# Attention with a routed MoE on one core: x and the high parts first, root chains ahead of v, unit loads in two transfers a head, and the later norms in steps 23 to 33

## What is computed

```python
x = L0_attn_x                                  # (4, 1024, 128), 16 heads of 8
xn = _layernorm(x, axis=-1)
# attention: one projection is query, key and value at once
p = jnp.einsum('bsd,ed->bse', xn, Wv) + bv     # q = k = v = p by heads
attn = softmax(q @ k.T / math.sqrt(8))
s = jnp.einsum('bsd,ed->bse', attn @ v, Wo) + bo
# ffn of xn: layernorm z (g, b), 8 experts, the best 2 of softmax(z @ rW + rb), weights renormalised
hid = gelu(z @ W1[e] + b1[e]); outs = hid @ W2[e] + b2[e]
ffn = xn + sum_e w[e] * outs[e]
out = x + s * silu(ffn)
```

## Time and profile before

| what | us |
|---|---|
| median of 3 runs | 629.17 |
| lowest, highest | 628.30, 630.58 |
| the profiled execution | 632.46 |
| its span, first to last instruction | 630.7 |
| busy: TensorE / ScalarE / VectorE / GpSimd | 571.2 / 543.2 / 240.1 / 230.1 |

### The profile page before, as it was taken

One profiled execution on the slowest core, in us unless ns is written; L12 is line 12 of the kernel. 1 busy time (PEld: TensorE's weight loads), 2 busy tenths in 40 slices (PEclk: granted clock), 3 DMA queues, 4 the chain that ended last, 5 costly groups with the idle time before them and its releaser, 6 DMA issues.

```text
span 630.7 us, 11527 instructions
## 1 busy us (share of the span) xinstructions
PE 571.2 (91%) x3990; PEld 232.3 (37%) x3990; DVE 240.1 (38%) x695; ACT 543.2 (86%) x591; POOL 230.1 (36%) x252
## 2 busy tenths in 40 slices
PE   3778884799999999799999999999988999999996
PEld 2553320223344344333444344434334343433221
DVE  5553863573333333113222232223232852223381
ACT  4576663699999999979999999999999999999994
POOL 2364047827777774254211121112203334341000
PEclk9977776799999999869999999999995999999999
DMA  6137697746466655227363445453233654442220
GB/s 164 45 101 219 231 304 276 184 132 149 110 162 133 162 96 116 70 67 160 68 153 99 127 112 132 103 135 108 70 117 108 173 167 139 130 116 83 65 66 19
DMA packets 100989, 81.54 MB, mean 129 GB/s; under 512 B 54219, under 2 KB 92638, under 8 KB 100318
## 3 DMA queue, kind: packets, MB, share of 16 engines
q1 hardware_dynamic: 94270, 71.26, 43.2%
q0 software_dynamic: 6656, 9.48, 4.8%
HBM read 58.07 MB, written 28.39 MB: 137 GB/s over the span
## 4 chain that ended last, share of the span: by engine, by line
PE 74%; ACT 9%; DVE 7%; issue 5%; DMA 4%; SPq 1%; ACTq 0%; DVEq 0%
PE bank_v L1330 35%; PE pair L1276 16%; PE bank_f L1370 8%; PE bank_f L1379 8%; ACT exps L776 7%; DMA p_dram<-w_ring 3%; PE bank_f L1347 2%; PE pair L1236 1%; ACT pre L752 1%; PE bank_f L1343 1%; PE pair L1227 1%; DMA x_tok<-in_L_attn_x 1%; DVE o_turned L1082 1%; PE bank_f L1354 1%; DVE v_tok L863 1%
## 5 line engine op out<-in xcount | busy, mean ns | idle before, releaser
L776 ACT ACTIVATE exps<-pair 128x1024 f32<-128x1024 f32 x512 | 488.9, 1049 | 54.6 <-PE pair L1276 36.3
L1330 PE MATMUL bank_v<-exps,v_tok 128*32 128x512 f32 x2048 | 285.0, 630 | 3.1 <-ACT exps L776 1.6
L687 POOL DMA_INDIRECT o_dram<-o_ring,slot_place x80 | 77.4, 968 | 238.3 <-DVE o_ring L1133 238.0
L1276 PE MATMUL pair<-q_ring,k_ring 26*128 26x512 f32 x1024 | 152.9, 513 | 2.7 <-ACT exps L776 2.1
L1276 PEld LDWEIGHTS pair<-q_ring,k_ring 26*128 26x128 f32 x1024 | 60.7, 188 | 93.4 <-ACT exps L776 54.8
L672 POOL DMA_INDIRECT z_dram<-pre,dest_i x64 | 64.3, 1004 | 52.2 <-DVE place_i L1037 33.3
L1379 PEld LDWEIGHTS bank_f<-w_ring,pre 128*128 128x128 f32 x320 | 46.2, 208 | 72.2 <-issue 43.3
L1124 DVE TENSOR_TENSOR pre<-bank_f,w_ring 128x256 f32<-128x256 f32 x80 | 33.9, 423 | 102.1 <-PE bank_f L1370 102.1
L1379 PE MATMUL bank_f<-w_ring,pre 128*128 128x128 f32 x320 | 62.5, 322 | 9.7 <-ACT pre L752 5.3
L1133 DVE TENSOR_TENSOR o_ring<-bank_f,w_ring 128x128 f32<-128x128 f32 x80 | 23.2, 290 | 124.3 <-PE bank_f L1379 121.1
L679 POOL DMA_INDIRECT place_dram<-token_place,place_i x64 | 61.3, 958 | 19.5 <-issue 19.5
(11 more groups left out here) (154 smaller groups left out, 287.1 us busy)
## 6 DMA issues: line engine op xcount, KB each, us to landing
w_ring<-w_dram SPq DMA_DIRECT2D x80, 192.0 KB
w_ring<-w_dram SPq DMA_DIRECT2D x80, 129.0 KB
q_ring<-p_dram SPq DMA_DIRECT2D x56, 104.0 KB
k_ring<-p_dram SPq DMA_DIRECT2D x56, 96.0 KB
z_dram<-s_tok SPq DMA_DIRECT2D x4, 1280.0 KB, 13.1
z_ring<-z_dram SPq DMA_DIRECT2D x80, 64.0 KB
rows_in_sb<-o_dram SPq DMA_DIRECT2D x16, 256.0 KB, 2.9
p_dram<-z_ring SPq DMA_DIRECT2D x8, 256.0 KB, 2.9
```

What stands on the lines that cost most here:

```text
L687: pool.indirect_dma_start(o_dram[:, :], bass.IndirectOffsetOnAxis(slot_place[:, h, 4 * k + i:4 * k + i + 1].bitcast(U32), 0), o_ring[:, q ...
L776: nc.scalar.activation(exps[:, g % ES, 2 * half:2 * half + 2, :], pair[(2 * g + half) % 3][:, :, :], ACT.Exp, scale=SCALE).then_inc(exp_do ...
L1276: ins = nc.tensor.matmul(pair[h % 3][:, j % 2, :], k_ring[32 * j:32 * j + KROWS, n % 2, kt * P:(kt + 1) * P], q_ring[32 * j:32 * j + KROWS ...
L1330: ins = nc.tensor.matmul(bank_v[32 * j:32 * j + 32, :], v_tok[:, (n // HG) * KT + kt, first:first + 32], exps[:, g % ES, j, :], start=(kt ...
```

## The change

SP loads x's third chunk ahead of the small weights. `sum_gram` takes no statistics between its operations, and the third `norm1` stands ahead of the first `keep_p`. `norm2` moves from between `keep_p(4)` and `keep_p(5)` to behind VectorE's branch, ahead of `keep_router_bias`. The second four warm-up matmuls go. For blocks 0 and 1 the high part is stored three times, straight into all its places, so the copy inside DRAM leaves out batch 0 and stands behind both `zero_z`. Units 0 and 1 are loaded with two transfers a head, behind the stores of blocks 3 and 4. The loads of rb, W1 and bo stand behind all stores of parts. The tables put the count in step 8, the biases in 9 to 16, the norms in 23, 25, ... 33, and the first `up` stays in step 38.

```diff
-WARM = (4, 4)
+WARM = 4
-RANK_AT = ((2, 3, 3, 4, 4, 5), (17, 18, 19, 20, 22, 23))
-COUNT_AT = (7, 24)
-ASSIGN_AT = ((7, 8, 8, 9, 10), (25, 26, 27, 28, 30))
+RANK_AT = ((3, 4, 4, 5, 5, 6), (17, 18, 19, 20, 22, 23))
+COUNT_AT = (8, 24)
+ASSIGN_AT = ((8, 9, 9, 10, 11), (25, 26, 27, 28, 30))
...
-BIAS_AT = 4
+BIAS_AT = 9
+COPY_HI_AT = 14
-NORM_AT = 12
-ZERO_AT = 12
-SCALE_W1_AT = (13, 14, 15, 16)
-SCATTER_AT = (11, 31)
-MOE_AT = 37
+NORM_AT = 23
+ZERO_AT = 8
+SCALE_W1_AT = (18, 19, 20, 21)
+SCATTER_AT = (12, 31)
+MOE_AT = 38
...
-        place(("norm", g), NORM_AT + g - EARLY)
+        place(("norm", g), NORM_AT + 2 * (g - EARLY))
...
             load_x(1)
+            load_x(2)
...
-                for part in range(PARTS):
-                    row = (HI_ROW, LO_ROW)[part]
-                    sp.dma_start(p_dram[:, row:row + DK, tokens], (p_hi, p_lo)[part][:, g % 2, :]).then_inc(parts_stored[g % 2], 16)
-                if g == EARLY:
+                hi_rows = (0, HI_ROW, LO_ROW + DK) if g < EARLY else (HI_ROW,)
+                for row in hi_rows:
+                    sp.dma_start(p_dram[:, row:row + DK, tokens], p_hi[:, g % 2, :]).then_inc(parts_stored[g % 2], 16)
+                sp.dma_start(p_dram[:, LO_ROW:LO_ROW + DK, tokens], p_lo[:, g % 2, :]).then_inc(parts_stored[g % 2], 16)
+                if g == 2:
...
+                elif g == 3:
...
-                    for j in range(4):
-                        load_head(0, 0, j, 0, kq_in[0])
-                        load_stabiliser(0, j, kq_in[0])
-                if g == 3:
-                    sp.dma_start(w1_stage, W1.rearrange("e h f -> h e f")).then_inc(w1_staged, 16)
-                    sp.dma_start(rb_bc[:, :], ...
-                    sp.dma_start(bo_bc[:, :], ...
+                    load_unit(0)
+                elif g == 4:
+                    load_unit(1)
+            sp.dma_start(rb_bc[:, :], ...
+            sp.dma_start(w1_stage, W1.rearrange("e h f -> h e f")).then_inc(w1_staged, 16)
+            sp.dma_start(bo_bc[:, :], ...
+            zero_z(0)
...
-            zero_z(0)
-            load_unit(1)
...
-                if g == 2:
+                if g == COPY_HI_AT:
                     for row in (0, LO_ROW + DK):
-                        sp.dma_start(p_dram[:, row:row + DK, :], p_dram[:, HI_ROW:HI_ROW + DK, :]).then_inc(hi_copied, 16)
+                        sp.dma_start(p_dram[:, row:row + DK, EARLY * BLK:], p_dram[:, HI_ROW:HI_ROW + DK, EARLY * BLK:]).then_inc(hi_copied, 16)
...
-                                             head_sel[:, :].unsqueeze(2).broadcast_to([P, H, DK]), ALU.mult), statistics)
+                                             head_sel[:, :].unsqueeze(2).broadcast_to([P, H, DK]), ALU.mult))
...
-            keep_p(0)
             norm1(2, *NORMS[2])
-            for g in range(1, NB):
+            for g in range(NB):
                 keep_p(g)
...
-                elif g == 4:
-                    norm2()
...
+            norm2()
             keep_router_bias()
...
-                keep_warm(WARM[1])
                 prologue()
```

More of the change, by code:

```diff
@@ L41 @@
 PARTS = 2
+EARLY_PARTS = 4
 PROWS = 3 * DK
@@ L58 @@
 PART_LOADS = 4 * 4
-KQ_FIRST = PART_LOADS + 4
+EXACT_LAST = PART_LOADS + 2 * 4
 KQ_LOADS = 4 * 2
@@ L388, in build, with stored @@
         out_rows = out.rearrange("b s d -> (b s) d")
+        def stored(g):
+            return 16 * (EARLY_PARTS + g // 2 * PARTS)
         def written(*use):
@@ L410, in _ @@
             sp.dma_start(rw_sb[:, :], rW).then_inc(small_in, 16)
-            for c in range(2, len(X_CHUNKS)):
+            for c in range(3, len(X_CHUNKS)):
                 load_x(c)
@@ L442, in load_stabiliser, with load_unit @@
                              p_dram[(n % HG) * 4 + j, M_ROW:HEAD_ROWS, tokens]).then_inc(loaded, 16)
+            def load_unit(n):
+                if n >= 2:
+                    sp.wait_ge(pv_done, (n - 1) * US)
+                if n == HG:
+                    sp.wait_ge(hi_copied, 32)
+                    for i in range(2):
+                        sp.wait_ge(m_kept[1 + i], (NB - EARLY) // 2 * 16)
+                tokens = slice((n // HG) * S, (n // HG + 1) * S)
+                for j in range(4):
+                    head = (n % HG) * 4 + j
+                    sp.dma_start(k_ring[32 * j:32 * j + PROWS, n % 2, :].bitcast(F32), p_dram[head, 0:PROWS, tokens]
+                                 ).then_inc(kq_in[n % 2], 16)
+                    sp.dma_start(q_ring[32 * j:32 * j + KROWS, n % 2, :].bitcast(F32), p_dram[head, HI_ROW:HEAD_ROWS, tokens]
+                                 ).then_inc(kq_in[n % 2], 16)
             for g in range(NB):
@@ L453, in _ @@
                         sp.dma_start(p_dram[:, M_ROW, e * BLK:(e + 1) * BLK], m_blk[:, e, :]).then_inc(m_kept[0], 16)
-                    for i in range(2):
-                        sp.wait_ge(parts_stored[i], 16 * PARTS)
+                elif g == 3:
+                    for e in range(EARLY):
+                        sp.wait_ge(parts_stored[e], stored(e))
                     sp.wait_ge(m_kept[0], 16 * EARLY)
@@ L458, in _ @@
                     sp.wait_ge(ring_cleared, 1)
-                    for j in range(4):
-                        load_head(0, 0, j, 0, kq_in[0])
-                        load_stabiliser(0, j, kq_in[0])
-                if g == 3:
-                    sp.dma_start(w1_stage, W1.rearrange("e h f -> h e f")).then_inc(w1_staged, 16)
-                    sp.dma_start(rb_bc[:, :], rb.rearrange("(a d) -> a d", a=1).broadcast_to([P, E])).then_inc(bias_in, 16)
-                    sp.dma_start(bo_bc[:, :], bo.rearrange("(a d) -> a d", a=1).broadcast_to([P, D])).then_inc(bias_in, 16)
+                    load_unit(0)
+                elif g == 4:
+                    load_unit(1)
+            sp.dma_start(rb_bc[:, :], rb.rearrange("(a d) -> a d", a=1).broadcast_to([P, E])).then_inc(bias_in, 16)
+            sp.dma_start(w1_stage, W1.rearrange("e h f -> h e f")).then_inc(w1_staged, 16)
+            sp.dma_start(bo_bc[:, :], bo.rearrange("(a d) -> a d", a=1).broadcast_to([P, D])).then_inc(bias_in, 16)
+            zero_z(0)
             for i in range(2):
-                sp.wait_ge(parts_stored[i], NB // 2 * 16 * PARTS)
+                sp.wait_ge(parts_stored[i], stored(NB - 2 + i))
             sp.wait_ge(m_row_ready, 1)
@@ L479, in _ @@
             with sp.If(m2_bits > M2_LIMIT_BITS):
-                sp.wait_ge(kq_in[0], 16 * KQ_FIRST)
+                for i in range(2):
+                    sp.wait_ge(kq_in[i], 16 * KQ_LOADS)
                 with sp.Fori(0, NU // 2) as w:
@@ L492, in _ @@
                     load_head(0, 0, j, 0, exact_in)
[L493 to L514 removed]
+                    for n in range(2):
+                        load_stabiliser(n, j, exact_in)
+                sp.wait_ge(exact_in, NU * 16 * PART_LOADS + 16 * EXACT_LAST)
             def load_w1(q):
@@ L656, in split @@
                 if g >= 2:
-                    pool.wait_ge(parts_stored[g % 2], g // 2 * 16 * PARTS)
+                    pool.wait_ge(parts_stored[g % 2], stored(g - 2))
                 pool.tensor_copy(hi.bitcast(F32R), src).then_inc(pool_chain, 1)
@@ L892, in beside_norm @@
                     keep_m2()
-                else:
-                    statistics()
+                statistics()
             for t in range(7):
```

29 lines of the change are left out of this document (4 added, 25 removed).

## The result

The changed kernel takes **644.03 us** (median of 4 runs, 641.55 to 644.75) against 629.04 us for the kernel before (4 runs, 628.3 to 630.58): a ratio of 1.0221 with a 95% interval of 1.0186 to 1.0255. It is slower by some 15 us, where 2 us faster was forecast, and outside the range of 618 to 634.5. Medians are of all executions; the ratios leave out three that took over 1.5% longer than the fastest of their kernel at a lower mean clock (two of e12's eleven, one of e9's six). The profiled execution took 644.17 us, its span is 642.4 us against 630.7, so the two traces lie 11.7 us apart; the other 3.3 us of the 15 are there because the profiled execution of the kernel before was 3.4 us over its median. 11.0 of the 11.7 us are there when the first expert product, up(0,0), starts. I read the trace along the same marks as before.

A forecast was written before the change was run, and what follows sets the result against it. Bound by 256 steps of two exponentials each, with gains only ahead of that; 21.8 us gained by step 29, mostly given back in SP's queue: 4.4 minus 2.4 leaves 2.0 us, so 627.2 us, range 618 to 634.5.

The forecast's parts named there:

- the stream behind norm 5: SP's in-order issues from VectorE's read of the last norm to up(0,0): 32.4 us, leaving TensorE waiting 16.3 us.
- how much there was to give back: The lead of the steps ahead of up(0,0): step 29 starts at 113.9 instead of 135.72, 21.8 us gained.
- rconst comes at 58.5: VectorE's router bias, waiting for bo_bc issued at 53 and landing in 5.6 us: 58.5 instead of 59.96.
- 19.5 us, and 2.4 us for the slow clock: Steps 9 to 16: eight bias uses at 2.44 us a step, plus slow clock and VectorE's long assign part.
- Steps 17 to 29: Twelve free steps (22.3 us), three norms at 0.38 us and 1 us for turn, projection and count: 24.4 us.
- the prologue: Ahead of the step loop: waits of ScalarE (4.81 us) and TensorE (4.63 us) go, step 0 starts at about 42.5.
- the lower bound that I had named: Gain at m2 from loading x sooner, put at 1.5 us: nothing if small loads land late behind x.
- the restart behind up(0,0): TensorE resumes at half clock after its wait for z_ring, costing 2.4 us.
- the warm-up: Prologue matmuls removed: transposes start at about 14.6 instead of 18.07; 2.08 us taken whole, about 1 by the skill's rule.
- up(0,0) after 155: Sign that the forecast is wrong and C or D holds: the first expert product starts later than 155 us.
- C: Rival: slower, SP's stream from norm 5's read to z outlasts the steps' lead; 632 to 634 us, chance 0.20.
- D: Rival: prologue does not move, four stores a slot hold GpSimd, bo_bc lands 3 us later; 630 to 632, chance 0.08.

The follow-up runs named there:

- e12: The changed kernel with the bias uses at steps 12 to 18 and 20 and W1's scaling at 21 to 24: 630.49 us over 11 runs, ratio 0.9993.
- e9: e5 with the bias uses at steps 12 to 18 and 20, W1's scaling and the w1 loads later: 606.50 us, ratio 0.9593.
- e1: The changed kernel with W2's copies and the places issued right behind the copy of the high parts (step 14): 630.00 us, ratio 0.9978.
- e5: The changed kernel with W2's copies, the places, rb and bo early, and w1 and z issued ahead of unit 3: 611.93 us, ratio 0.9707.
- e2: The changed kernel with the loads of rb and bo issued ahead of block 0's parts: 634.20 us, ratio 1.0054.
- e7: The changed kernel with W2's copies, the places, rb and bo early, and the matmuls of the eight bias uses left out: 612.81 us.
- e11: e5 with the bias uses at every second step (10 to 22, then 25), W1's scaling and w1 loads later: 610.46 us, ratio 0.9693.
- e13: The same kernel as e12, run under a second name for a second trace, whose execution took 632.22 us.
- e8: The changed kernel with the norms back at steps 17, 18, 20, 22, 23, 25: 632.53 us, ratio 1.0015.
- e14: e9 with m_blk's stores behind block 1's parts and unit 0's loads behind block 2's: 604.86 us, ratio 0.961.

## Why the prediction was wrong, step by step

**Right: the stream behind norm 5.** Forecast 32.4 us from VectorE's read of norm 5 to up(0,0); measured 165.68 - 132.34 = 33.3. Forecast 16.3 us of wait, 12 to 20; measured 19.6. e1 and e5 show that it is SP's order, and what each piece of it costs. The late norms were named as what gives the gain back, and they are.

**Wrong: how much there was to give back.** up(0,0) was put at 150.2 and came at 165.68, 15.5 us late. The wait for norm 5's read (4.9 us behind the start of step 29 instead of 3.9) and the stream (33.3 instead of 32.4) are 1.9 of these; the rest is there before them: step 29 was put at 113.9 and came at 127.43. Three terms make up the 13.5 us.

*"rconst comes at 58.5"*: 64.54, 6.0 late. I had seen that keep_router_bias waits for bo_bc, put its issue at 53 (57.4) and its landing at 5.6 us (7.1, with the stores and W1 in front of it). e2 confirms that it was this load: bo early brings rconst at 55.56. The count followed, 73.3 instead of 67.6: **5.7 us**.

*"19.5 us, and 2.4 us for the slow clock"*: from the count to step 17 I took 21.9 us, at 2.44 a step; it took 28.6. **6.7 us.** The duration of a bias use, 0.61, came from a row at full speed, and the slow clock was priced as a restart that ends in a few microseconds, as the earlier trace rows showed it twice. In those two restarts no bias uses stood. e7, e9, e11 and the pair e12 and e13 show what I lacked: once the clock had fallen, it didn't come back in steps that each had such a use. The trace of before had the other size as well, which the prediction leaves out: its bias uses at 69.48 and 87.16 took 1.01 us.

*Steps 17 to 29*: 25.5 instead of 24.4: **1.1 us**, steps 17 to 20 still at the lower clock.

**Wrong: the prologue.** Step 0 came at 46.95 instead of 42.5. The prediction moved the third root chain ahead of all copies of v and took its 4.81 us as won; that the first copy of v now waits for that chain, and TensorE for the copy, it put at nothing. The trace shows the wait, and that GpSimd starts block 2 late for ScalarE's output behind it:

```profile
26.33 1.97 PE L1237 MATMUL pair<-wv_rw,pre 128*128 128x136 f32 x8 [3.95 <-DVE lg_all L868]
```

```profile
31.66 1.04 POOL L659 TENSOR_TENSOR w_ring<-zT 128x512 bf16<-128x512 f32 x1 [4.33 <-ACT zT L741]
```

The four stores of slot 0, which by the prediction held split(2) so that it ended at 31, held nothing in the trace (L662 follows L659 at once). Block 2's stores came at 34.6, unit 0's loads at 38.9 to 42.4, 3.5 us later than put, and they landed 4 us behind. By the order of GpSimd and SP this delay goes on to block 7's stores, so I take it for most of the 4.4 us by which bo's load was issued late, and thus inside the 5.7 us above; no run tests it alone. In e8, whose prologue is the same, the wait for VectorE was 2.46 us instead of 3.95, bo's load was issued at 54.92 and rconst came at 62.31. m2 was not earlier either: the small loads behind x came late (bv's transpose at 6.73 instead of 5.24), the lower bound that I had named. e14 shows that a step 0 at 41.8 brings the count 3.6 us forward, and the total by nothing that can be measured.

**Wrong by its size, and luck: the restart behind up(0,0)** was put at 2.4 us. From the start of up(0,0) to the end of the span the changed kernel took 476.7 us and the one before 476.1, so it was 0.7. That made the miss of the span 13.7 us instead of 15.5. The median missed by 16.8 (644.03 against 627.2), since the prediction took off 3.3 us, by which the profiled execution of before lay over its median, while that of the changed kernel (644.17) lay on its median.

**Right: the warm-up.** The first transposes started at 16.07 instead of 17.86 (the 18.07 of the prediction is the modelled end of the warm-up), and the clock was not lost by it: the 512-column matmuls, 2.08 us for two at 20.55 before, read here

```profile
18.52 1.64 PE L1228 MATMUL pair<-pre,wv_rw 128*128 128x512 f32 x2
...
21.36 1.02 PE L1228 MATMUL pair<-pre,wv_rw 128*128 128x512 f32 x2
```

full speed from about 20, earlier than before. (These are read from the durations; the granted clock in the rows says 1.00 there in both traces, and is of use only later. It fell to 0.50 at about 27, behind the 3.95 us of wait, for some 3 us.) In e5, which has the same prologue but for bo's load, full speed came only at about 22.5, still not later than the 24 of the kernel before. By what the Trainium skill says of activity and the clock (TensorE: Matmul & The Clock Gate, Part 1), the edit would be worth 1 us by the prediction's estimate, where its sum took 2.08. The transposes came 1.8 us earlier, and neither trace shows a later rise of the clock. The page's closing table advises the warm-up for benchmarks.

**The rivals.** By the prediction's own sign, up(0,0) after 155, the answer is C or D. C had the direction, and 632 to 634; its break-even of 34.4 us of stream, against 33.3, was not even passed. The lead over the kernel before was 8.3 us instead of 21.8, and the stream ate all of it and 11 more. D was right that bo_bc lands late (6 us, not 3), but not by its cause, and step 0 did move. No rival had the clock. The 0.74 for "faster" or "same" hung on terms worked out at full speed.

## What to carry to other kernels

A duration has a clock: before a row's time is multiplied by a number of steps, see at which level it was taken and at which the new steps will run. Here small matmuls in a row were best placed where TensorE already ran at full speed, some steps behind a stall (e9 against e5); whether the clock had risen before the first of them was 14 us at up(0,0) (e12, e13). And an in-order DMA queue is a schedule: moving the wait (a norm's store) behind other steps moves everything that is issued after it; first put what waits for nothing (W2's copies) in the queue's idle time. Four such edits on the same change (W2's copies, bo, w1 and z, the bias uses) gave 606 us instead of 644.
